# A transformer block with a routed feed-forward on one core: gathers issued in groups, and a new order of the opening steps

## The chip, the core and the metric

One core of one Trainium2 chip runs the whole program. The metric is device time in microseconds: from the start of the execution to its end, median of the runs. The profiler's page and trace come from one further execution.

## The reference, cut to what matters

Everything is float32. One layer on x (2048 rows of 512): two branches, each behind a layer norm that a modulation vector scales and shifts; all six modulation vectors come from one 512 x 3072 product.

```python
mod = (silu(c) @ wmod).reshape(1, 6, 1, 512)
sa, ca, ga, sb, cb, gb = mod[:, 0], ..., mod[:, 5]
ga = (2 * (ga >= 0) - 1) * maximum(abs(ga), 0.25)      # gb alike
h = layernorm(x) * (1 + ca) + sa
x = x + ga * (tanh(h @ B.T) @ C.T + D * h)             # 256 states
h = layernorm(x) * (1 + cb) + sb
scores = sigmoid(h @ gate_w.T)                         # 8 experts
# top 2 of scores + bias, weights normalised over the two
y = sum over the two experts of w * (silu(h @ W1) * (h @ W3)) @ W2   # 352 wide
x = x + gb * (y + shared)                              # shared: the same form, 704 wide
```

## The kernel before

**Precision.** Each float32 product is made of three TensorE passes on a high part (ScalarE's copy into the `hi` tile, type fp32r) and a low part (VectorE's or GpSimd's value minus high part, the `lo` tile): high by high, high by low, low by high. So each operand costs one ScalarE copy and one subtraction before TensorE can use it.

**Tiling.** The 2048 rows are 16 tiles of 128, worked in 8 pairs. `iterations` runs a software pipeline over `it`; at `it` the engines work on pair `it` (statistics, normalising: `first_stats`, `first_aggr`, `first_root`, `normalise`), on pair `it - 1` (transposes of the normalised tile `tbuf`: `turn_t` on TensorE, high part `turned` on ScalarE, low part `turned_low` on VectorE, then `states`), on pair `it - 2` (`attention`, which is the product with C; residual sum, second layer norm, giving `h2`), and on pair `it - 3` (transposes of `h2`, high part `high_a`, low part `lows_a`, then the first half of the shared expert: `up`, SiLU in `hidden`, product `gbuf` in `product_a`, transposes of `gbuf` in `turn_g`, high and low part `gth` and `gtl`, `down`). The term with D is added to x by GpSimd (`times_d`, `with_d`). The parameter `lo` of each `body` is the iteration's number where it is written out (0 to 4 and the last ones), so conditions such as `lo == 3` single out one of them. `body(3)` is the first with all four stages.

**Opening.** Ahead of `body(3)` each engine has its own list. TensorE forms the six modulation vectors (`modulation(0)` to `(5)`, the last in PSUM bank 7) between the first pairs' transposes, states and attention. The shared expert's weights come in three pieces: W1/W3 in two (`first_weights(0)`, `(1)`) and W2 (`first_weights(2)`), which GpSimd first multiplies by gb (L698). `guard(5)` forms that gb: VectorE takes the sign from PSUM (L1282), ScalarE the magnitude (`magnitude`), and VectorE joins them (L1285). The router's weights are 32 columns, high part L890 on ScalarE, low part L1624 on VectorE; TensorE's first `up` waits for them.

**The later stages.** Stage A's rows are scattered by expert. Stage B gives the shared expert's other half to the last four tiles, stage S takes the routed tiles through their experts (results to `ys_rows` in HBM), and stage C gives the shared expert's other half to the other 12 tiles. Each `step` is: `up`, `down` of the tile before, transposes of `gbuf`. In C each tile's two routed rows are fetched by two indirect DMAs from GpSimd (`gather`, into `tbuf` and `xtf`), with indices that VectorE makes (`offsets`) once the place is free. The six tiles that went through the shared half elsewhere or come last (`FIRST_LAST`) have their rows fetched beside, by `gather_first`, into `rowb`; ScalarE weighs the first row (`weigh`, at the steps in `WEIGH_AT`), and VectorE does three operations for each (`combine`, parts 0 to 2, at the steps in `COMBINE_AT`, numbered 3 * tile + part). The queue of each engine is in program order: a wait in it holds all that stands behind.

Of the kernel before, what the change touches and what calls it, by code (L numbers as in the profile page):

```python
# [39 lines left out]
UP = 2 * F  # L40
# [23 lines left out]
WEIGH_AT = [2, 4, 5, 7, 8, 10]  # L64
COMBINE_AT = [(), (), (), (0, 1), (2,), (3, 4), (5, 6), (7, 8), (9, 10), (11, 12), (13, 14), (15, 16)]
# [17 lines left out]
def build(nc, x, ccol, wmod, bt, ct, dvec, gwt, rb, w_all, consts, out):  # L83
# [6 lines left out]
    with ExitStack() as ctx:  # L90
# [223 lines left out]
        def pairs_of_b(eng):  # L314

            return eng.value_load(ti[0:1, TB_ITERS:TB_ITERS + 1], min_val=NP - 2, max_val=SMAX // 2 - 2) + 2

# [219 lines left out]
        def _(pool):  # L537
# [75 lines left out]
            def body(it, lo, hi):  # L613
# [87 lines left out]
            with_d(2)  # L701
# [60 lines left out]
        def _(act):  # L762
# [14 lines left out]
            def hidden(p, j, lo):  # L777
                n = p * 2 + (j + 1)
                act.wait_ge(q["A", "up"], n)
                if lo > 3 or j:  # L780
# [3 lines left out]
                               ACT.Copy).then_inc(s_lg, 1)  # L784
                if lo == NP + 1 and j == 1:
# [20 lines left out]
            def turned(p, lo):  # L806
# [3 lines left out]
                for j in range(2):  # L810
                    act.activation(thi[:, :, j * P:j * P + P],
                                   bank[2 + j][:, :].rearrange("p (k m) -> p k m", k=KD),
# [130 lines left out]
        def _(pe):  # L943
# [38 lines left out]
            def up(sec, i, j, off, there=None, loaded=None, apart=False):  # L982
# [13 lines left out]
                for m, h in [(m, h) for h in range(2) for m in range(KD)] if apart else [  # L996
# [4 lines left out]
                    if True:  # L1001
                        if sec == "A":
                            w, n = m * UPA + h * (E + F), F + (1 - h) * E
                        else:
                            w, n = off + (SH + m * UP + h * F), F
                        wh, wl = whi[:, bass.ds(w, n)], wlo[:, bass.ds(w, n)]
                        dst = bank[2 + h][:, 0:n]
# [845 lines left out]
```

## Time and profile before

| | us |
|---|---|
| median of 3 runs | 557.76 |
| lowest, highest | 556.29, 557.81 |
| the profiled execution | 561.89 |
| its span, first to last instruction | 560.2 |
| TensorE busy in it | 542.0 |
| VectorE, GpSimd, ScalarE busy | 291.0, 262.8, 176.8 |
| TensorE's mean granted clock | 0.994 of full |

The profiled execution is one of its own and need not equal the median. A row of the timeline gives start, length, engine, line of the kernel, operation, the tiles written and read, the count, and in brackets how long the engine stood idle before and what released it. The ends of matmuls are modelled. "Issue" as a releaser means nothing that the profile shows. PE is TensorE, DVE VectorE, ACT ScalarE, POOL GpSimd, SP SyncE.

### The profile page before, as it was taken

Reading aid. Unit: us, or ns where it says so; the run is one execution under the profiler, and the core shown is the slowest. Engines: PE = TensorE matmul, PEld = TensorE weight load, DVE = VectorE, ACT = ScalarE, POOL = GpSimd, SP = SyncE. Lnnn points to the kernel's source line nnn. Section 1 sums busy time; section 2 is a strip of 40 time slices with the busy share of each in tenths; the row PEclk is TensorE's granted clock in tenths of the full one; section 3 lists DMA queues with packets and bytes.
Section 4 is the critical chain, followed back from the end, with each engine's and each line's share of the span. In section 5 each row is a group of like instructions: output and inputs, shape, how many; then the busy total and the mean of one; then the engine's idle time right before and its main releaser. Section 6 shows DMA issues by size and latency. Waiting matters only on the chain.

```text
span 560.2 us, 11029 instructions
## 1 busy us (share of the span) xinstructions
PE 542.0 (97%) x3129; PEld 485.9 (87%) x3130; DVE 291.0 (52%) x612; ACT 176.8 (32%) x337; POOL 262.8 (47%) x221
## 2 busy tenths in 40 slices
PE   8997899999999999999999999999999999979997
PEld 3666888998999999899999999999999999958996
DVE  3787886696677657732222222222222221257887
ACT  1444435445443432122222223222233222112121
POOL 2499877667667457443054350053434200346530
PEclk9997999999999999999999999999999999999999
DMA  8999266543543397576354946265666413568952
GB/s 305 397 349 383 98 216 254 189 140 123 187 150 150 135 331 269 201 271 222 111 191 135 340 140 238 75 210 192 252 210 250 131 66 123 166 205 286 312 179 75
DMA packets 45676, 115.62 MB, mean 206 GB/s; under 512 B 4560, under 2 KB 4816, under 8 KB 45648
## 3 DMA queue, kind: packets, MB, share of 16 engines
q1 hardware_dynamic: 32848, 62.83, 31.9%
q0 software_dynamic: 12800, 52.43, 27.1%
q8 instruction: 16, 0.26, 0.2%
q14 instruction: 12, 0.10, 0.0%
HBM read 78.28 MB, written 36.96 MB: 206 GB/s over the span
## 4 chain that ended last, share of the span: by engine, by line
PE 88%; DVE 4%; another core or an unknown queue 2%; issue 2%; ACT 1%; DMA 1%; SPq 0%; DVEq 0%; ACTq 0%
PE bank L1010 15%; PE bank L1008 15%; PE bank L1009 15%; PE bank L1039 8%; PE bank L1041 8%; PE bank L1040 8%; PE bank L979 5%; PE bank L1046 4%; PE bank L948 3%; PE bank L949 3%; PE bank L950 3%; PE bank L957 3%; DMA x_all<-wmod 1%; DVE gtl L1301 1%
## 5 line engine op out<-in xcount | busy, mean ns | idle before, releaser
L1008 PE MATMUL bank<-whi,thi 128*128 (+2 forms) x368 | 122.8, 334 | 0.0
L580 POOL TENSOR_TENSOR wlo<-raw,whi 128x1408 f32 (+3 forms) x24 | 79.8, 3338 | 91.6 <-DMA whi<-w_all 80.7
L1009 PE MATMUL bank<-wlo,thi 128*128 (+2 forms) x368 | 119.6, 325 | 0.0
L1010 PE MATMUL bank<-whi,tlo 128*128 (+2 forms) x368 | 119.1, 324 | 0.0
L1740 DVE TENSOR_TENSOR gbuf<-s,bank 128x352 f32<-128x352 f32 x52 | 27.1, 521 | 105.2 <-ACT s L922 102.7
L1039 PE MATMUL bank<-whi,gth 128*128 (+1 forms) x201 | 79.8, 397 | 1.5 <-issue 1.5
L1041 PE MATMUL bank<-whi,gtl 128*128 (+1 forms) x201 | 79.1, 393 | 0.0
L1040 PE MATMUL bank<-wlo,gth 128*128 (+1 forms) x201 | 78.8, 392 | 0.0
L1758 DVE TENSOR_TENSOR gtl<-bank,gth 128x384 fp32r<-128x384 f32 x51 | 28.4, 557 | 84.4 <-ACT gth L929 81.3
L922 ACT ACTIVATE s<-bank 128x352 f32<-128x352 f32 x52 | 24.2, 466 | 149.8 <-PE bank L1010 143.8
L1008 PEld LDWEIGHTS bank<-whi,thi 128*128 128x128 f32 x368 | 69.7, 189 | 0.0
L1009 PEld LDWEIGHTS bank<-wlo,thi 128*128 128x128 f32 x368 | 69.1, 188 | 0.1
L1010 PEld LDWEIGHTS bank<-whi,tlo 128*128 128x128 f32 x368 | 69.1, 188 | 0.0
L929 ACT ACTIVATE gth<-bank 128x384 fp32r<-128x384 f32 x51 | 25.1, 492 | 105.7 <-PE bank L1046 97.2
L1008 PE MATMUL bank<-whi,xah 128*128 128x352 f32 (+2 forms) x176 | 58.3, 331 | 0.1
L1009 PE MATMUL bank<-wlo,xah 128*128 128x352 f32 (+2 forms) x176 | 57.2, 325 | 0.0
L1010 PE MATMUL bank<-whi,xal 128*128 128x352 f32 (+2 forms) x176 | 57.1, 325 | 0.0
L1041 PEld LDWEIGHTS bank<-whi,gtl 128*128 128x128 f32 x201 | 37.8, 188 | 8.9
L1039 PEld LDWEIGHTS bank<-whi,gth 128*128 128x128 f32 x201 | 37.9, 189 | 7.5 <-issue 1.8
L1040 PEld LDWEIGHTS bank<-wlo,gth 128*128 128x128 f32 x201 | 37.8, 188 | 5.8
L738 POOL DMA_INDIRECT tbuf<-ys_rows,idx x10 | 11.2, 1115 | 61.0 <-issue 44.3
L1046 PEld LDWEIGHTS bank<-cst,gbuf 128*128 128x128 f32 x204 | 25.7, 140 | 16.0 <-DVE gbuf L1740 4.3
(224 smaller groups left out, 984.5 us busy)
## 6 DMA issues: line engine op xcount, KB each, us to landing
raw<-w_all POOLq DMA_DIRECT2D x8, 2176.0 KB
whi<-w_all POOLq DMA_DIRECT2D x16, 704.0 KB, 11.4
h<-xs_rows SPq DMA_DIRECT2D x36, 256.0 KB, 2.8
ys_rows<-tmpa SPq DMA_DIRECT2D x36, 256.0 KB, 2.0
x_all<-wmod SPq DMA_DIRECT2D x6, 1024.0 KB, 9.3
whi<-w_all POOLq DMA_DIRECT2D x8, 768.0 KB, 5.3
hs_rows<-h SPq DMA_DIRECT2D x8, 512.0 KB, 4.9
mods<-hs_rows SPq DMA_DIRECT2D x7, 512.0 KB
```

The lines of the kernel that those rows point to most:

```text
L580: pool.tensor_tensor(wlo[:, bass.ds(off + (SH + a), b - a)], raw[:, a:b], whi[:, bass.ds(off + (SH + a), b - a)].bitcast(F32), ALU.subtrac ...
L929: act.activation(gth_b if last else gth[:, :], bank[4][:, 0:FP], ACT.Copy).then_inc(q["S", "ghi"], 1)
L979: mm = pe.transpose(dst[:, k * P:(k + 1) * P], src[:, k * P:(k + 1) * P], ident)
L1008: pe.matmul(dst, xh[:, j, a], wh, start=(m == 0), stop=False)
L1009: pe.matmul(dst, xh[:, j, a], wl, start=False, stop=False)
L1010: mm = pe.matmul(dst, xl[:, j, a], wh, start=False, stop=(m == KD - 1))
L1039: pe.matmul(dst, gth[:, a], wh, start=(m == 0), stop=False)
L1040: pe.matmul(dst, gth[:, a], wl, start=False, stop=False)
L1041: mm = pe.matmul(dst, gtl[:, a], wh, start=False, stop=(m == KF - 1))
L1046: mm = pe.transpose(dst[:, m * P:(m + 1) * P], gbuf[:, m * P:(m + 1) * P], ident)
L1740: dve.tensor_tensor(gbuf[:, 0:F], s1[:, :], bank[3][:, 0:F], ALU.mult).then_inc(q["S", "g"], 1)
L1758: dve.tensor_tensor(gtl_b if last else gtl[:, :], bank[4][:, 0:FP], (gth_b if last else gth[:, :]).bitcast(F32), ALU.subtract).then_inc(q[ ...
```

## The change

In stage C the gathers of rows (`gather_first`) are issued in the groups of `ROWS_AT`: none ahead of the first loop step, then after each tile's own gathers two, two, one, one, two, one, one and two of them, each group behind a wait for the transposes of `gbuf` of a step of stage C. `WEIGH_AT` and `COMBINE_AT` are moved one step later, and the last tile's part 1 goes into the last step, so parts 1 and 2 stand behind the last subtraction and `finish_last(0, 0, 1)`.

In the opening: on TensorE, `h2`'s transposes and the attention of pair 1 stand ahead of the transposes of pair 2, which go to banks 6 and 7 instead of 2 and 3 and wait for the states and for gb's sign and magnitude. On ScalarE, the router's high part comes before the states of pair 1, `high_a(0)` ahead of `normalise(2)`, pair 2's high part behind, and the SiLU of the first tile ahead of W2's high part. On VectorE, `h2` of pair 0 comes ahead of W1's second low part, `lows_a(0)` next, pair 3's statistics behind the first `gbuf`, `gtl` and the second `gbuf` ahead of `slo`. On GpSimd, `with_d(2)` moves from ahead of `body(3)` to behind its roots.

```diff
-WEIGH_AT = [2, 4, 5, 7, 8, 10]
-COMBINE_AT = [(), (), (), (0, 1), (2,), (3, 4), (5, 6), (7, 8), (9, 10), (11, 12), (13, 14), (15, 16)]
+WEIGH_AT = [3, 4, 6, 7, 9, 10]
+COMBINE_AT = [()] * 4 + [(n, n + 1) for n in range(0, 16, 2)]
+ROWS_AT = [(0, 1), (2, 3), (4,), (5,), (6, 7), (8,), (9,), (10, 11)]
...
+        def t_bank(lo, j):
+
+            return bank[6 + j] if lo == 3 else bank[2 + j]
@@ gpsimd @@
+                if lo == 3:
+                    with_d(2)
                 if lo > 2 and live(0, lo, hi):
                     times_d(it)
...
             times_d(2)
-            with_d(2)
             iterations(pool, body, 3)
...
             for j in range(2):
                 gather(CB, j)
-            for k in range(2):
-                gather_first(0, k)
             for c in range(CB + 1, NP - 1):
                 for j in range(2):
                     gather(c, j)
-                    n = (c - CB - 1) * 2 + j + 1
-                    if n < NB + NL:
-                        for k in range(2):
-                            gather_first(n, k)
+                    n = (c - CB - 1) * 2 + j
+                    turned_there = value(pool, iters * 2 + (NB + n + 3))
+                    pool.wait_ge(s_bidx, 2)
+                    pool.wait_ge(q["S", "gt"], turned_there)
+                    for m in ROWS_AT[n]:
+                        gather_first(m // 2, m % 2)
@@ scalar @@
+                if lo == 3 and j == 0:
+                    first_weights(2)
...
-                if live(1, lo, hi):
+                if live(1, lo, hi) and lo != 3:
                     turned(it - 1, lo)
                 if live(3, lo, hi):
                     p = it - 3
-                    if lo < NP + 2:
+                    if 3 < lo < NP + 2:
                         high_a(p, lo)
+                    if lo == 3:
+                        turned(it - 1, lo)
                     if lo > NP:
                         scores(p - 1)
-                    if lo == 3:
-                        first_weights(2)
                     hidden(p, 0, lo)
...
             modulation(4)
+            act.wait_ge(l_gate, 32)
+            act.activation(whi_a[:, :, 0:E], gw[:, :, :], ACT.Copy).then_inc(s_gwh, 1)
             states(1, 2)
+            high_a(0, 3)
             normalise(2)
             magnitude(5)
-            act.wait_ge(l_gate, 32)
-            act.activation(whi_a[:, :, 0:E], gw[:, :, :], ACT.Copy).then_inc(s_gwh, 1)
@@ tensor @@
+                if lo == 3:
+                    pe.wait_ge(s_tanh, p * 2)
+                    pe.wait_ge(s_sign, 2)
+                    pe.wait_ge(s_abs, 2)
+                for j in range(2):
+                    mm = transposes(t_bank(lo, j), tbuf[:, j, :])
...
-                if live(1, lo, hi):
+                if live(1, lo, hi) and lo != 3:
                     turn_t(it - 1, lo)
...
                 if live(2, lo, hi):
                     attention(it - 2, lo)
-
+                if lo == 3:
+                    turn_t(it - 1, lo)
...
-                    if live(1, lo, hi):
+                    if live(1, lo, hi) and lo > 3:
                         pe.wait_ge(s_tlo, (it - 1) * 2 + 2)
@@ vector @@
-                if live(3, lo, hi) and lo < NP + 2:
+                if live(3, lo, hi) and 3 < lo < NP + 2:
                     lows_a(it - 3, lo)
+                if lo == 3:
+                    turned_low(it - 1, lo)
...
                 if lo == 3:
+                    first_stats(it, lo)
+                    first_aggr(it, lo)
                     first_weights(2)
                 between(1)
+                if lo == 3:
+                    low_a(it - 3, 0, lo)
...
                     if lo == 2:
-                        first_weights(1)
                         dve.wait_ge(s_modc, 4)
...
+                if lo == 3:
+                    product_a(it - 3, 1, lo)
                 if live(1, lo, hi):
                     states_low(it - 1)
-                if live(3, lo, hi):
+                if live(3, lo, hi) and lo > 3:
                     product_a(it - 3, 1, lo)
...
             body(2, 2, 2)
-            guard(5, sign5[:, :], s_gb)
+            sign_of(5, sign5[:, :])
+            lows_a(0, 3)
+            first_weights(1)
             dve.wait_ge(l_gate, 32)
             dve.wait_ge(s_gwh, 1)
             dve.tensor_tensor(wlo_a[:, :, 0:E], gw[:, :, :], whi_a[:, :, 0:E].bitcast(F32),
                               ALU.subtract).then_inc(s_gwl, 1)
+            guard(5, sign5[:, :], s_gb)
             link(dve.memset(gbuf[:, F:FP], 0.0))
             body(3, 3, 3)
...
                     dve.wait_ge(q["S", "dn"], i * 2 + j)
                     finish_last(0, 0, 1)
-                    combine(NB + NL - 1, 2)
+                    for part in (1, 2):
+                        combine(NB + NL - 1, part)
```

`sign_of` is the first half of the old `guard`; `turned` and `turned_low` read `t_bank` too.

## Rows read from the trace of the kernel before

**Rows 1.** The page, part 1: busy time, share of the span, instructions.

```profile
PE 542.0 (97%) x3129; PEld 485.9 (87%) x3130; DVE 291.0 (52%) x612; ACT 176.8 (32%) x337; POOL 262.8 (47%) x221
```

**Rows 2.** TensorE's timeline, opening: start, length, engine, line, operation [idle before].

```profile
46.37 1.94 PE L979 MATMUL bank<-cst,tbuf 128*128 128x128 f32 x8 [3.82 <-issue]
...
53.73 0.33 PE L1008 MATMUL bank<-whi,xah 128*128 128x360 f32 x1
...
59.01 0.52 PE L1046 MATMUL bank<-cst,gbuf 128*128 128x128 f32 x3 [1.20 <-DVE gbuf L1297]
```

**Rows 3.** GpSimd's timeline in the opening.

```profile
30.91 3.64 POOL L689 TENSOR_TENSOR x_all<-x_all,tmpa 128x1024 f32<-128x1024 f32 x1
...
40.43 1.09 POOL L623 TENSOR_TENSOR rs<-ve,mhalf 128x2 f32<-128x2 f32 x1
...
47.23 2.69 POOL L596 TENSOR_TENSOR x_all<-x_all,tmpa 128x1024 f32<-128x1024 f32 x1
...
58.56 2.39 POOL L596 TENSOR_TENSOR x_all<-x_all,tmpa 128x1024 f32<-128x1024 f32 x1
```

**Rows 4.** Busy time by stretch; after POOL: TensorE's granted clock, DMA share, GB/s.

```profile
42.54:46.37 3.83, 0.01 (x2) 0.04 (x1) 2.48 (x4) 1.63 (x3) 3.61 (x6) 0.88 1.05 402
46.37:52.20 5.83, 5.83 (x22) 5.35 (x23) 5.31 (x7) 2.67 (x6) 5.75 (x3) 0.50 1.05 365
```

**Rows 5.** TensorE's timeline in stage C.

```profile
478.62 0.49 PE L1046 MATMUL bank<-cst,gbuf 128*128 128x128 f32 x3
...
484.89 0.49 PE L1046 MATMUL bank<-cst,gbuf 128*128 128x128 f32 x3
...
488.94 0.32 PE L1010 MATMUL bank<-whi,tlo 128*128 x1
...
493.01 0.55 PE L1046 MATMUL bank<-cst,gbuf 128*128 128x128 f32 x3 [1.67 <-issue]
...
502.31 0.55 PE L1046 MATMUL bank<-cst,gbuf 128*128 128x128 f32 x3 [0.95 <-DVE gbuf L1740]
...
547.35 0.49 PE L1046 MATMUL bank<-cst,gbuf 128*128 128x128 f32 x3
```

**Rows 6.** The chain of waits in order of time, 484 to 503.

```profile
485.52 6.39 another core or an unknown queue
...
492.40 5.23 another core or an unknown queue
```

**Rows 7.** GpSimd's timeline, the first and last of ten gathers in one run.

```profile
483.35 1.03 POOL L738 DMA_INDIRECT tbuf<-ys_rows,idx  x1 [41.60 <-issue]
...
495.41 0.95 POOL L744 DMA_INDIRECT raw<-ys_rows,idxb  x1 [0.30 <-issue]
```

**Rows 8.** VectorE's timeline in the opening.

```profile
34.96 1.25 DVE L1509 TENSOR_TENSOR x_all<-bank,x_all 128x512 f32<-128x512 f32 x2
...
38.14 0.25 DVE L1530 BATCH_NORM_AGGREGATE mv<-bn 128x2 f32<-128x6 f32 x2
...
40.88 1.61 DVE L1433 TENSOR_TENSOR wlo<-raw,whi 128x1408 fp32r<-128x1408 f32 x1
...
46.86 0.84 DVE L1285 SCALAR_TENSOR_TENSOR mods<-mods,sign 128x512 f32<-128x512 f32 x1 [1.83 <-ACT mods L871]
47.62 2.35 DVE L1624 TENSOR_TENSOR wlo<-gw,whi 128x32 fp32r<-128x32 f32 x1
...
50.04 1.29 DVE L1441 TENSOR_TENSOR tlo<-bank,thi 128x512 fp32r<-128x512 f32 x2
...
58.78 3.78 DVE L1433 TENSOR_TENSOR wlo<-raw,whi 128x1536 fp32r<-128x1536 f32 x1
```

**Rows 9.** DMA issues 480 to 560: count, KB each, median us to landing.

```profile
raw<-ys_rows,idxb POOLq DMA_INDIRECT x8, 5.3
```

**Rows 10.** VectorE's timeline at the end.

```profile
555.69 0.68 DVE L1685 TENSOR_TENSOR mods<-mods,x_all 128x512 f32<-128x512 f32 x1
```

More of the change, by code:

```diff
@@ L811, in turned @@
                     act.activation(thi[:, :, j * P:j * P + P],
-                                   bank[2 + j][:, :].rearrange("p (k m) -> p k m", k=KD),
+                                   t_bank(lo, j)[:, :].rearrange("p (k m) -> p k m", k=KD),
                                    ACT.Copy).then_inc(s_thi, 1)
@@ L1000, in up @@
                         pe.wait_ge(w_ready, there[m // (KD // 2)])
[L1001 to L1007, printed above, removed]
-                        pe.matmul(dst, xh[:, j, a], wh, start=(m == 0), stop=False)
-                        pe.matmul(dst, xh[:, j, a], wl, start=False, stop=False)
-                        mm = pe.matmul(dst, xl[:, j, a], wh, start=False, stop=(m == KD - 1))
+                    if sec == "A":
+                        w, n = m * UPA + h * (E + F), F + (1 - h) * E
+                    else:
+                        w, n = off + (SH + m * UP + h * F), F
+                    wh, wl = whi[:, bass.ds(w, n)], wlo[:, bass.ds(w, n)]
+                    dst = bank[2 + h][:, 0:n]
+                    pe.matmul(dst, xh[:, j, a], wh, start=(m == 0), stop=False)
+                    pe.matmul(dst, xh[:, j, a], wl, start=False, stop=False)
+                    mm = pe.matmul(dst, xl[:, j, a], wh, start=False, stop=(m == KD - 1))
                     if apart and h == 0 and m == KD - 1:
@@ L1059, in turn_t @@
                     pe.wait_ge(s_lg, (p - 3) * 2 + 2)
+                if lo == 3:
+                    pe.wait_ge(s_tanh, p * 2)
+                    pe.wait_ge(s_sign, 2)
+                    pe.wait_ge(s_abs, 2)
                 for j in range(2):
-                    mm = transposes(bank[2 + j], tbuf[:, j, :])
+                    mm = transposes(t_bank(lo, j), tbuf[:, j, :])
                 mm.then_inc(s_tT, 1)
@@ L1277, in _, with sign_of @@
                 dve.tensor_scalar(silb[k], const("ones"), sil[:, k:k + 1], None, ALU.mult).then_inc(s_silb, 1)
+            def sign_of(i, sign):
+                dve.wait_ge(s_mod, i + 1)
+                dve.tensor_scalar(sign, bank[MBANK[i]][:, :], 0.0, 0.5, ALU.is_ge, ALU.subtract).then_inc(s_sign, 1)
             def guard(i, sign, done):
-                g, m = bank[MBANK[i]][:, :], mods[:, WM[i], :]
-                dve.wait_ge(s_mod, i + 1)
-                dve.tensor_scalar(sign, g, 0.0, 0.5, ALU.is_ge, ALU.subtract).then_inc(s_sign, 1)
+                m = mods[:, WM[i], :]
                 dve.wait_ge(s_sign, 1 if i == 2 else 2)
@@ L1440, in turned_low @@
                     t = slice(j * P, (j + 1) * P)
-                    dve.tensor_tensor(tlo[:, :, t], bank[2 + j][:, :].rearrange("p (k m) -> p k m", k=KD),
+                    dve.tensor_tensor(tlo[:, :, t], t_bank(lo, j)[:, :].rearrange("p (k m) -> p k m", k=KD),
                                       thi[:, :, t].bitcast(F32), ALU.subtract).then_inc(s_tlo, 1)
@@ L1494, in between @@
                         route(it - 4, lo, *which)
-                if live(1, lo, hi) and lo > 1:
+                if live(1, lo, hi) and lo > 1 and lo != 3:
                     turned_low(it - 1, lo)
-                if live(3, lo, hi) and lo < NP + 2:
+                if live(3, lo, hi) and 3 < lo < NP + 2:
                     lows_a(it - 3, lo)
+                if lo == 3:
+                    turned_low(it - 1, lo)
                 if lo == 2:
@@ L1509, in body @@
                         dve.tensor_tensor(xt, bank[j][:, :], xt, ALU.add).then_inc(s_x1, 1)
-                if live(0, lo, hi) and lo != 2:
+                if live(0, lo, hi) and lo not in (2, 3):
                     first_stats(it, lo)
@@ L1520, in body @@
                 if live(0, lo, hi):
-                    if lo != 2:
+                    if lo not in (2, 3):
                         first_aggr(it, lo)
@@ L1571, in body @@
                     normalise(it, lo)
+                if lo == 3:
+                    product_a(it - 3, 1, lo)
                 if live(1, lo, hi):
                     states_low(it - 1)
-                if live(3, lo, hi):
+                if live(3, lo, hi) and lo > 3:
                     product_a(it - 3, 1, lo)
@@ L1606, in _ @@
             ins.then_inc(s_blo, 1)
+            sign_of(2, mods[:, 5, :])
             guard(2, mods[:, 5, :], s_ga)
```

## The prediction

> **What bounds the kernel now.** I read the page first: TensorE is busy for 542.0 of 560.2 us [rows 1], so the end moves only where TensorE waits, runs at the low clock, or has finished. The waits of TensorE and its timeline then show three such places.
>
> First the opening. TensorE stands still for 3.82 us before the transposes of pair 2 at 46.37, which wait for the normalised tile from ScalarE, and that for GpSimd's small operations behind the root that ends at 41.52 [rows 2, 3]. The granted clock falls within that idle stretch (0.88 on average) and is 0.50, the 1.2 GHz level, over 46.37 to 52.20 [rows 4]. Then come 1.20 us of waiting for the first gbuf [rows 2]. A second place is the start of the tail stage C, where results are gathered and combined. One of its steps, from the transposes of one tile's hidden row to the next one's, takes 484.89 - 478.62 = 6.27 us; the two after that take 17.42 instead of 12.54, and all ten up to 547.35 take 68.73 instead of 62.7 [rows 5]. So 4.88 us are lost in two steps and 1.15 in the other eight. The chain of waits names no engine: 6.39 and 5.23 us stand under "another core or an unknown queue" [rows 6]. The last matmul of the first product was recorded at 488.94 to 489.26 [rows 5], but ScalarE, which waits for its semaphore, went on only when that first piece ended, at 491.91. In that stretch GpSimd issues ten gathers back to back, 483.35 to 496.36 [rows 7]. The third place is the last few microseconds, VectorE's own.
>
> **The change, opening.** The sum follows the port that VectorE and GpSimd fight for. An operation of VectorE on two SBUF tiles does not run beside one of GpSimd's: the router weights' low part, 32 columns, took 2.35 us and ended at 49.97, when GpSimd's 2.69 us addition at 47.23 had ended (49.92); W2's low part took 3.78 us and ended 1.62 us after GpSimd's addition at 58.56 did [rows 3, 8]. The other way round, GpSimd's addition took 3.64 us at 30.91 where 2.39 is usual [rows 3].
>
> Step 1: h2 of pair 0 no longer waits behind W1's second low part (1.61 us, 40.88 to 42.49) [rows 8], but only for GpSimd's root at 41.52 [rows 3]. It ends some 0.8 us sooner, near 43.0, and slo follows. TensorE ends the last modulation at 42.55 and so waits about 0.4 us, then has the transposes of h2 and the attention of pair 1 to do. That cover of 4 us is what fills the 3.82 us. Pair 2's transposes come third. Even at the low clock all three blocks took 53.73 - 46.37 = 7.36 us [rows 2], so TensorE is ready for the first up product by 43.0 + 7.4 = 50.4.
>
> Step 2: what that product then waits for is the router weights' low part. GpSimd's small operations end up to 0.6 us sooner, as VectorE holds the port less. The D term in two parts follows, and near 47.23 - 0.6 = 46.6 both want the port: GpSimd for the 2.4 us addition, VectorE for W1's low part (1.61), which now stands there. If VectorE goes first, the addition ends at 46.6 + 1.5 + 2.4 = 50.5; if GpSimd does, the low part ends at 49.0 + 1.6 = 50.6. Either way the router's low part is there near 50.5. If it slipped in before the addition it would be 48.2, and 50.5 is the end that the row of 2.35 us is nearest to. So the product starts near 50.6 against 53.73.
>
> The Trainium skill (SBUF — State Buffer, section "Who interferes with whom") calls this an exclusive lock held for the whole instruction, with whoever starts first the winner. That speaks against the placing, because the guard of gb, moved behind the weights, reads two SBUF tiles too. By the rule it starts after the addition and the opening gains what step 3 gives; were the port only shared, router's part and guard would be done by 49.1, the addition near 50.5 would set the pace, and the opening would gain 4.4.
>
> Step 3: VectorE is now the late one. From 50.5: guard 0.84 [rows 8], low part of pair 2's transposes 1.29, then residual, statistics and aggregation of pair 1, 34.96 to 38.39 = 3.43 in the same order [rows 8]. That is 56.1. The first up product took 53.73 to 57.81 = 4.1 us [rows 2], so it ends near 54.7 and the SiLU is ready at 55.2, hidden by VectorE. gbuf takes 0.52, and the transposes of it begin near 56.7 instead of 59.01 [rows 2]: **2.3 us gained**. The wait in front of them grows from 1.2 to about 2.0 us.
>
> Step 4: is it kept? Statistics of pair 3 (1.5 us) precede W2's low part; that now meets only GpSimd's small operations, since its D addition has moved behind them: 1.6 us instead of 3.78, ending near 60. ScalarE's W2 high part needs W2 scaled, which starts with the guard (51.4) and takes 3.5: 54.9, after the SiLU, hence the new order of these two. With the old order the SiLU would be 1.5 us late. The down product stands 7 us behind the transposes of gbuf and so is not reached before 63.8. The D addition ends near 66 and is first needed at about 71. SP's store of h2 and the two loads of x are issued at the same waits. Nothing of this is late, so 2.3 us are kept. Bounds: 4.5 gained (router's part at 48.2 and the guard with it), 1 lost (below, the clock).
>
> **The change, stage C.** The gathers of rows start one step later, each waits for a transposed gbuf, and they are spread over eight steps (2, 2, 1, 1, 2, 1, 1, 2) instead of six twos. So the first run of ten becomes four, a pause of 2 us for tile 2's indices, four, and four more. The waits sit on GpSimd's queue behind the tile's own gathers; the next tile's indices come from VectorE some 4.4 us after that same transposition, and two row gathers take 2.5, so no tile gather is held up. A gather's landing takes 5.3 us [rows 9]; the weighing on ScalarE sits behind it in front of the next SiLU. For the first row pair, issued near 493.2 and 494.5 on the old clock, it lands at 499.8, is weighed by 500.6, and the SiLU is due at 501.6: 1 us of cover, and about as much for the others. If that cover is gone, a SiLU is late by the excess.
>
> What the calmer issue is worth the trace of before does not show. Lower end: nothing, if the lateness of the semaphores is not of the gathers. Upper end: all 6.0 us. Later, with eight gathers in a run with one short pause, steps lost only 1.15 us in eight, and the new pattern is nearest to that: two steps would lose 0.3 to 0.9 instead of 4.88, so 4.0 gained. But the profiled execution took 561.89 us (1.69 around the span), 4.13 above the median of 557.76, and this stall is the likeliest thing to be smaller without it. I take 2.5.
>
> **The end.** The last tile's second part moves behind the last subtraction: one more operation of 0.68 us [rows 10] in VectorE's chain, on the path to the last store. One is taken from no other place on the path. **0.7 us lost.** The rest costs nothing on the path: the sign is only taken apart from the guard, and the router's high part on ScalarE (32 columns) falls while TensorE still forms the states that ScalarE needs next. If its load landed late, ScalarE would hold the states of pair 1 for as long, and h2's transposes with it.
>
> **Sum.** In the profiled execution: 561.89 - 2.3 - 4.0 + 0.7 = 556.3. For the timed runs: 557.76 - 2.3 - 2.5 + 0.7 = 553.7.
>
> **The rivals.**
> (a) The stall of stage C stays, as it is not of the run of gathers; only the opening gains. For it: no engine is named, and eight later gathers in one run did little harm. Against it: the step before the gathers takes its 6.27 us and the first two with them 17.42. 557.76 - 2.3 + 0.7 = 556.2, at the edge of what counts.
> (b) The stall goes wholly in the timed runs too, and the router's part slips in early: 557.76 - 4.5 - 4.9 + 0.7 = 549.1; with the stall alone gone, 551.3.
> (c) Slower: the low clock moves. TensorE now has waits of 0.4, 0.5, 2.2 and 2.0 us within 14 us where it had 3.8 and 1.2. If the clock falls in the 2.2 us in front of the first up product, that product takes 8.2 instead of 4.1 us and part of the next block its double: about 5.5 us against the 2.3, so 3.2 lost in the opening. It decides only if the fall comes there and stage C gives nothing: 557.76 + 3.2 + 0.7 = 561.7. Waits of up to 1.67 us in stage C left the clock at full; 3.82 did not [rows 2, 5]. The 2.2 lies between.
> (d) The weighing comes late: a row gather lands 2 us later than the median once its queue is full, six times, each 1 us past its cover. Then SiLUs give back the gain: about 558.
>
> **How the numbers follow.** The forecast, opening kept and stage C better by 1 to 4 us, gets 0.45 and gives 552 to 555.5. (a) gets 0.24, (b) 0.12, (c) 0.07, (d) and other orderings that turn out no better 0.12. What this kernel's measurement can tell from no change is 0.3%, or 1.7 us: faster means under 556.1. The forecast and (b) are faster, and nearly half of (a): 0.67. Within: the rest of (a) and half of (d): 0.20. Slower, above 559.4: (c) and half of (d): 0.13. The range 549.8 to 558.6 leaves out the best of (b), (c) and the worst of (d).
>
> **What would show it.** In the profile after: TensorE's order of h2, attention, pair 2, with no idle stretch above 2.5 us near 42 to 57 and the granted clock at 1.00 there; the router's low part ending with GpSimd's addition, near 50.5; the first gbuf transposes near 56.7 (58 or later proves step 3 wrong, 54.6 proves the lock wrong). In stage C: steps of about 6.3 us from the first on and no piece of 5 us under an unknown queue; if these pieces stand while gathers are fewer, (a) is right. At the end, eight operations of VectorE after the last subtraction where seven were, 0.7 us longer. The prediction fails if the clock falls before the first up product, or if ScalarE waits for a row's landing.

## The result, and the profile of the changed kernel

The changed kernel takes **553.61 us** (553.57 to 556.34, 6 runs) against 557.78 (556.29 to 559.44, 6 runs) for the kernel before on the same chip: a ratio of 0.9946, 95% interval 0.9931 to 0.9961. Timed again with the experiments below it gave 553.57 (0.9933, 0.992 to 0.9946). The forecast was 553.7. The sum hit the total, and that is luck: two of its terms were each wrong by over 2 us, in opposite directions. Most of what follows is about that.

| | us |
|---|---|
| profiled execution, its span | 556.34, 554.6 |
| TensorE busy in it | 540.5 |
| VectorE, GpSimd, ScalarE busy | 293.1, 263.0, 176.5 |
| mean granted clock | 0.995 |

The changed kernel's runs fall in two groups, and the profiled one is of the upper: spans of about 551.9 with a granted clock of 0.999 or 1.0 (four of six), and about 554.6 at 0.995 (two of six).

TensorE's timeline in the opening, every entry that has an idle time ahead of it (start, length, engine, line, operation, [idle before <- releaser]):

```profile
43.58 1.06 PE L988 MATMUL bank<-cst,h 128*128 128x128 f32 x8 [0.61 <-issue]
47.80 1.07 PE L988 MATMUL bank<-cst,tbuf 128*128 128x128 f32 x8 [0.34 <-ACT mods L879]
50.55 0.42 PE L1016 MATMUL bank<-whi,xah 128*128 128x360 f32 x1 [1.68 <-issue]
57.42 0.52 PE L1054 MATMUL bank<-cst,gbuf 128*128 128x128 f32 x3 [1.20 <-DVE gbuf L1312]
69.80 1.06 PE L988 MATMUL bank<-cst,h 128*128 128x128 f32 x8 [1.80 <-DVE gtl L1316]
```

The idle stretch of 3.82 us [rows 2] is gone, and the first up product starts at 50.55 instead of 53.73. But it is followed by the low clock, which takes most of the gain in this execution (busy time by stretch; behind POOL the granted clock):

```profile
50.50:54.20 3.70, 3.65 (x13) 3.69 (x14) 3.56 (x7) 0.00 (x0) 3.07 (x1) 0.54 1.01 384
```

VectorE's timeline in the opening, the lines that answer to [rows 8]:

```profile
48.11 2.33 DVE L1649 TENSOR_TENSOR wlo<-gw,whi 128x32 fp32r<-128x32 f32 x1
50.37 0.68 DVE L1300 SCALAR_TENSOR_TENSOR mods<-mods,sign 128x512 f32<-128x512 f32 x1
...
55.10 0.25 DVE L1547 BATCH_NORM_AGGREGATE mv<-bn 128x2 f32<-128x6 f32 x2
56.76 0.52 DVE L1312 TENSOR_TENSOR gbuf<-s,bank 128x352 f32<-128x352 f32 x1 [1.41 <-ACT s L788]
...
58.73 1.73 DVE L1448 TENSOR_TENSOR wlo<-raw,whi 128x1536 fp32r<-128x1536 f32 x1
...
62.35 3.45 DVE L1583 SCALAR_TENSOR_TENSOR h<-h,rs,mods 128x512 f32<-128x512 f32 x2
...
66.16 2.43 DVE L1472 TENSOR_TENSOR slo<-st,shi 128x512 fp32r<-128x512 f32 x1
```

And GpSimd's: the last addition of pair 1's D term, and the first two operations of pair 2's (`with_d(2)`, which the change moves here):

```profile
46.78 3.61 POOL L601 TENSOR_TENSOR x_all<-x_all,tmpa 128x1024 f32<-128x1024 f32 x1
...
62.26 3.00 POOL L598 TENSOR_TENSOR tmpa<-tmpa,a 128x512 f32<-128x512 f32 x2
```

W2's low part takes 1.73 us where it took 3.78. The last two of VectorE's lines are new: two operations on SBUF tiles that take 3.45 and 2.43 us beside GpSimd's moved D term, where the same operations took 1.41 and 0.68 in the kernel before. They will matter.

Stage C on TensorE, the first and the last of ten steps and the one with a delay:

```profile
478.00 0.49 PE L1054 MATMUL bank<-cst,gbuf 128*128 128x128 f32 x3
484.26 0.49 PE L1054 MATMUL bank<-cst,gbuf 128*128 128x128 f32 x3
...
503.22 0.55 PE L1054 MATMUL bank<-cst,gbuf 128*128 128x128 f32 x3
...
541.05 0.49 PE L1054 MATMUL bank<-cst,gbuf 128*128 128x128 f32 x3
```

The ten steps take 541.05 - 478.00 = 63.05 us, not the 68.73 of the kernel before (547.35 - 478.62) [rows 5]. No piece of the chain stands under "another core or an unknown queue". In this pair of profiles the change thus saves 0.6 us by the start of stage C (478.62 - 478.00), 5.7 in its ten steps, and loses 0.7 at the end: 5.6, as the spans say (560.2 - 554.6). That looks like a success of the gathers. It isn't, as the experiments show.

### The profile page after: what moved, and what is told of

Its sections match the earlier page's. It is cut to its first block, busy times and chain, and to the rows that moved or that the text cites. A ratio compares the mean times of both kernels' runs of the same rounds, so it can differ in the third digit from the quotient of the medians.

```text
span 554.6 us, 11046 instructions
## 1 busy us (share of the span) xinstructions
PE 540.5 (97%) x3129; PEld 485.6 (88%) x3130; DVE 293.1 (53%) x612; ACT 176.5 (32%) x337; POOL 263.0 (47%) x221
## 3 DMA queue, kind: packets, MB, share of 16 engines
q1 hardware_dynamic: 32848, 62.83, 32.3%
## 4 chain that ended last, share of the span: by engine, by line
PE 83%; DVE 5%; issue 1%; ACT 1%; DVEq 0%
PE bank L1016 15%; PE bank L1017 15%; PE bank L1018 15%; PE bank L1047 8%; PE bank L1049 8%; PE bank L1048 8%; PE bank L1054 4%; PE bank L988 4%; PE bank L957 2%; PE bank L959 2%; PE bank L958 2%; DVE gtl L1316 1%; DVE st L1669 0%; DVE slo L1472 0%; ACT gth L800 0%
## 5 line engine op out<-in xcount | busy, mean ns | idle before, releaser
L1016 PEld LDWEIGHTS bank<-whi,thi 128*128 128x128 f32 x368 | 69.8, 190 | 0.0
L556 POOL DMA_DIRECT2D whi<-w_all x21 | 11.4, 552 | 54.8 <-PE bank L1018 54.7
```

What stands on the lines that cost most here:

```text
L1016: pe.matmul(dst, xh[:, j, a], wh, start=(m == 0), stop=False)
```

## The experiments

In what follows "first" and "second gbuf" are the transposes of gbuf for the two tiles of pair 0, "h2 of pair 1" the transposes after them, "ten steps" the stretch read from [rows 5].

**The two halves apart.** First the new opening with the old order of gathers and sums, then the old opening with the new one, the kernel before once more, and the changed kernel with the first row pair gathered ahead of the loop again.

```diff
# e1_opening_only: the changed kernel, with
-WEIGH_AT = [3, 4, 6, 7, 9, 10]
-COMBINE_AT = [()] * 4 + [(n, n + 1) for n in range(0, 16, 2)]
+WEIGH_AT = [2, 4, 5, 7, 8, 10]
+COMBINE_AT = [(), (), (), (0, 1), (2,), (3, 4), (5, 6), (7, 8), (9, 10), (11, 12), (13, 14), (15, 16)]
...
# the old loop of gather_first and the old last step; e2_gathers_only: the reverse, on the kernel before
# e4_first_pair_back: the changed kernel, with
-ROWS_AT = [(0, 1), (2, 3), (4,), (5,), (6, 7), (8,), (9,), (10, 11)]
+ROWS_AT = [(), (2, 3), (4,), (5,), (6, 7), (8,), (9,), (10, 11)]
             for j in range(2):
                 gather(CB, j)
+            for k in range(2):
+                gather_first(0, k)
```

> The changed kernel with stage C as before: the opening alone. Theory (the two parts add up, and stage C gave 5.7 us in the profile): stage C's ten steps take about 68.7 us again, the time is 555.5 to 558, about 1 us under before. Rival (the opening gives most of what the timed runs gained, and the stall of stage C was the profile's): 553.5 to 554.5, and stage C near 63 us in most executions.

> The kernel before with the new gathers, weighing and combining alone. Theory: stage C's ten steps take 63.0 us, the end 0.7 us more, so 5.0 us less in the profile; in the timed runs 3 to 5 us under before. Rival (the stall is hardly there in timed runs): within 1 us of before.

> The kernel before, as it was, to see each execution's span and granted clock. If the low clock in the opening comes and goes, spans fall in groups about 2 to 3 us apart with mean clocks near 0.994 and 1.0. If the stall of stage C is there in each execution, the profile has it again (ten steps 68 to 69 us); if it comes and goes, this profile may show about 63.

> The changed kernel, but the first pair of row gathers stands ahead of the loop again, so six to eight gathers are issued in one run at the start of stage C. Theory (the length of that first run makes TensorE's semaphores late): the pieces under an unknown queue are back, stage C's ten steps take 67 to 69 us, 4 to 5 us slower than the changed kernel. Rival (the number of row gathers in later steps, or something else, is the cause): stage C stays near 63 us and the time near 553.6.

| | us | runs | ratio to before, 95% interval | ten steps in its profile |
|---|---|---|---|---|
| before, beside them | 557.52 | 20 | | |
| e1, opening alone | 552.87 | 5 | 0.994 (0.9916 to 0.9964) | 62.83 |
| e2, gathers alone | 558.55 | 10 | 1.0021 (1.0008 to 1.0034) | 63.38 |
| e3, before again | 557.41 | 10 | 0.9996 (0.9986 to 1.0005) | 62.83 |
| e4, first pair back | 553.31 | 4 | 0.9931 (0.9914 to 0.9948) | 62.83 |

The opening alone gives the whole gain and more: 4.65 us. The new gathers alone cost 1.0. The kernel before, profiled again, has its run of ten gathers and no stall at all: 62.83 in ten steps. So the stall of 4.88 us belonged to the one execution that had been profiled first, 4.13 us above its median. Over all thirteen later profiles the ten steps take 62.83 to 63.80, and eight of these have the old run of ten gathers. That the gathers can never bring such a stall is not shown; that they don't bring it in a usual execution is. e4 says the same from the other side: with eight gathers in one run at the start of the changed kernel, where 67 to 69 us were expected in ten steps, these take 62.83.

The second profile of before (557.29 us, near the median) also shows another opening than the first. TensorE:

```profile
46.42 1.94 PE L979 MATMUL bank<-cst,tbuf 128*128 128x128 f32 x8 [3.82 <-issue]
57.70 0.52 PE L1046 MATMUL bank<-cst,gbuf 128*128 128x128 f32 x3 [1.20 <-DVE gbuf L1297]
66.25 0.47 PE L1039 MATMUL bank<-whi,gth 128*128 128x512 f32 x1 [1.23 <-DVE gtl L1301]
69.28 0.55 PE L1046 MATMUL bank<-cst,gbuf 128*128 128x128 f32 x3 [0.67 <-DVE gbuf L1297]
71.09 1.06 PE L979 MATMUL bank<-cst,h 128*128 128x128 f32 x8 [0.40 <-DVE gtl L1301]
```

VectorE and GpSimd beside it:

```profile
57.48 2.68 DVE L1433 TENSOR_TENSOR wlo<-raw,whi 128x1536 fp32r<-128x1536 f32 x1
60.08 3.55 DVE L1547 SCALAR_TENSOR_TENSOR h<-x_all,mv,mods 128x512 f32<-128x512 f32 x2
64.22 1.41 DVE L1563 SCALAR_TENSOR_TENSOR h<-h,rs,mods 128x512 f32<-128x512 f32 x2 [0.59 <-POOL rs L623]
```

```profile
58.62 3.79 POOL L596 TENSOR_TENSOR x_all<-x_all,tmpa 128x1024 f32<-128x1024 f32 x1
```

And the opening alone (e1), on TensorE:

```profile
50.50 0.40 PE L1015 MATMUL bank<-whi,xah 128*128 128x360 f32 x1 [1.69 <-issue]
55.85 0.52 PE L1053 MATMUL bank<-cst,gbuf 128*128 128x128 f32 x3 [1.20 <-DVE gbuf L1311]
66.83 1.06 PE L987 MATMUL bank<-cst,h 128*128 128x128 f32 x8 [0.39 <-DVE gtl L1315]
```

By the first gbuf the gain is 57.70 - 55.85 = 1.85 us; by h2 of pair 1 it is 71.09 - 66.83 = 4.26. So 2.4 us, more than half, come between the two. As the rows read, the kernel before loses them there to GpSimd's D term: W2's low part takes 2.68, the first half of h2 3.55 where 1.41 is usual, the root behind the addition is awaited, and gtl, last in VectorE's queue, reaches TensorE 1.23 us late.

The first profile of before, the one that the prediction was made from, doesn't have this loss. Its h2 of pair 1 follows the first gbuf (59.01) by 10.97 us, as in e1 (10.98), not by 13.39:

```profile
69.98 1.06 PE L979 MATMUL bank<-cst,h 128*128 128x128 f32 x8 [0.39 <-DVE gtl L1301]
```

There the low clock had lasted twice as long, and VectorE came to W2's low part at 58.78, when GpSimd had just started its addition at 58.56 [rows 3, 8]. It lost to it once (3.78 us), and both halves of h2 then took 1.4 each. In e3 it came at 57.48, 1.3 us sooner, met GpSimd twice, and h2 of pair 1 was 1.1 us later for it. So in the kernel before a fall of the clock in the opening costs little or nothing: of its executions timed beside the experiments, the two with a granted clock of 1.0 took 557.25 and 557.28, and the fastest (556.1 to 556.7) all had 0.993 or 0.994, as the first profile with its long low stretch.

**Is the moved D term what gives the 2.4 us?** From here on the base is e1, and the kernel before beside these runs took 557.75 (19 runs).

```diff
# e5_d_term_back
-                if lo == 3:
-                    with_d(2)
...
             times_d(2)
+            with_d(2)
             iterations(pool, body, 3)
```

> The new opening with the old stage C (as in the opening alone, 552.87 us), but GpSimd adds pair 2's D term ahead of its roots again. Theory (the moved D term is worth about half of the opening's gain, since W2's low part, h2 of pair 1 and the D term then fight for one port): the second tile's down product or gbuf waits again, 1 to 2 us together, h2's transposes of pair 1 come 1.5 to 3 us later than 66.8, time 554.4 to 556. Rival (the new order of TensorE's blocks gives all of it): 552.6 to 553.2.

Measured 559.53 (558.51 to 560.22, 8 runs; ratio 1.0033, 1.0021 to 1.0044): 6.7 us above e1 (6.4 if each is taken against the kernel before beside it), 3.5 above the upper end of what was expected, and slower than the kernel before. The wait moved to the second gbuf, on TensorE:

```profile
70.42 0.55 PE L1052 MATMUL bank<-cst,gbuf 128*128 128x128 f32 x3 [3.38 <-DVE gbuf L1310]
```

On GpSimd the addition at 60.01 takes 3.79 us and everything for pair 1's root stands behind it until 65.6; behind that wait TensorE ran at the low clock again. With two falls of the clock in the profile, 6.7 is not the price of the place beside VectorE alone. But the direction is plain: without this edit the new order loses.

**The router's low part first.** 

```diff
# e6_router_early
             sign_of(5, sign5[:, :])
-            lows_a(0, 3)
-            first_weights(1)
             dve.wait_ge(l_gate, 32)
             dve.wait_ge(s_gwh, 1)
             dve.tensor_tensor(wlo_a[:, :, 0:E], gw[:, :, :], whi_a[:, :, 0:E].bitcast(F32),
                               ALU.subtract).then_inc(s_gwl, 1)
+            lows_a(0, 3)
+            first_weights(1)
```

> The new opening with the old stage C, and the low part of the router's weights ahead of the two low parts of h2 on VectorE. Theory (VectorE's chain behind the guard sets the first gbuf, not the router's part): the first up product starts near 49 instead of 50.5, and the transposes of gbuf stay within 0.3 us of 55.85; time 552.6 to 553.3, or up to 2.5 us more if the longer wait in front of those transposes takes the clock down. Rival (the router's part sets it): 1.5 us faster, about 551.3.

Measured 554.53 (554.51 to 555.1, 4 runs; 0.9951, 0.9934 to 0.9968). The up product now starts without a wait, 2.2 us earlier (48.26), and the first gbuf only 0.33 earlier:

```profile
55.52 0.64 PE L1053 MATMUL bank<-cst,gbuf 128*128 128x128 f32 x3 [3.10 <-DVE gbuf L1311]
```

So a sooner up product alone doesn't bring the first gbuf; VectorE's chain, from the end of GpSimd's addition to the aggregation, holds it, as step 3 of the prediction had it. (e12 will add that a sooner VectorE alone doesn't bring it either.) And the whole wait in one piece, 3.10 us, is followed by the low clock, which the 1.20 of e1 was not:

```profile
55.70:59.20 3.50, 3.50 (x19) 3.50 (x18) 3.41 (x7) 0.58 (x2) 3.42 (x4) 0.51 0.37 136
```

**The states of pair 2 in the wait.**

```diff
# e7_states_first
+                if lo == 3:
+                    states(it - 1, lo)
...
-                if live(1, lo, hi):
+                if live(1, lo, hi) and lo != 3:
                     states(it - 1, lo)
```

> The new opening with the old stage C, and on TensorE the states of pair 2 ahead of the transposes of the first gbuf, in the time in which it waits for them. Theory (that wait of 1.20 us is on the path and nothing behind it becomes late): the wait is gone, 1.0 to 1.3 us faster, 551.6 to 551.9, and the low clock comes less often. Rival (VectorE and GpSimd set the pace behind it as well): the wait shows up at the second gbuf or at h2 of pair 1 instead, 552.6 to 553.

Median 554.24 of ten runs (0.995, 0.9926 to 0.9974), in three groups: five at 552.4 to 552.9 with the clock at 0.999 or more, two at 555.6 to 555.8 (0.996), three at 556.5 to 557.2 (0.994). The best are 0.3 us under e1's, where 1.0 to 1.3 were expected. The wait moved to the second gbuf (0.92 us at 64.64), and the falls of the clock are no rarer (five of ten runs, against two of five). Filling this wait gives next to nothing, as VectorE is late again one tile on.

**SiLU behind W2's high part, as before.**

```diff
# e8_w2_before_silu
-                if lo == 3 and j == 0:
-                    first_weights(2)
...
+                    if lo == 3:
+                        first_weights(2)
                     hidden(p, 0, lo)
```

> The new opening with the old stage C, but ScalarE makes W2's high part ahead of the first SiLU again. Theory (it waits for GpSimd's scaled W2 until 54.6 and then takes 1.5): the SiLU comes at 56.1 instead of 54.7, the first gbuf's transposes 1.2 us later than 55.85, time 553.9 to 554.2. Rival (VectorE is late anyway): within 0.3 us of 552.87.

Measured 555.47 (555.24 to 555.97, 6 runs; 0.9964, 0.9951 to 0.9976), 2.6 above e1. The first gbuf is 1.28 us later (57.13, behind 2.58 us of waiting), as expected; but 553.9 to 554.2 were expected for the time. The clock is low from 58.16 on, and the rest of the loss is the meeting described under e12.

**The chain shortened.** e6, with the first gbuf taken ahead of pair 1's statistics.

```diff
# e9_gbuf_before_stats: e6, with
                         dve.tensor_tensor(xt, bank[j][:, :], xt, ALU.add).then_inc(s_x1, 1)
+                if lo == 3:
+                    product_a(it - 3, 0, lo)
...
-                if live(3, lo, hi):
+                if live(3, lo, hi) and lo > 3:
                     product_a(it - 3, 0, lo)
# e12_gbuf_first_alone: e1, with the same edit
```

> Base: the new opening with the old stage C, 552.87 when timed. Two edits: the router's low part ahead of pair 0's low parts on VectorE, as in the run of that edit alone (554.53, transposes of the first gbuf at 55.52 behind a wait of 3.10 us for gbuf, which drew a fall of the clock), and the first gbuf ahead of the statistics of pair 1 instead of behind them. My theory: VectorE's chain sets the first gbuf transposes, 1.5 us of it being those statistics, and the length of the wait in front of them decides whether the clock falls. Then gbuf is formed at about 53.3 us, as soon as its SiLU is there, its transposes begin near 54.0 with a wait of 1.3 us, the clock stays at full in most runs, and the time is 551.0 to 552.4. The rival: what is late afterwards is h2 of pair 1, whose statistics come 0.6 us later, and the next product's weights; TensorE only waits there instead, 552.6 to 554.5.

```profile
53.93 0.52 PE L1053 MATMUL bank<-cst,gbuf 128*128 128x128 f32 x3 [1.38 <-DVE gbuf L1311]
```

**552.12 us** (551.96 to 552.24, 4 runs) against 557.5 (11 runs): 0.9904, 0.9889 to 0.9918. It is the best of the kernels, 1.45 us under the changed kernel beside it, and its granted clock was 0.999 or 1.0 in every run. The same edit without the router's:

> Base: the new opening with the old stage C (552.87 when timed, two of five runs near 555.2 with the granted clock at 0.996). One edit: the first gbuf ahead of the statistics of pair 1 on VectorE. With the router's low part ahead as well, this gave 552.12 and no fall of the clock in the opening. Theory: the falls come from the wait of 1.69 us in front of the first up product, and that wait is still here, so some of the runs still stand 2.3 to 2.7 us higher, with a low stretch that begins within 0.5 us of that product's start; at full clock the first gbuf transposes stay within 0.3 us of 55.85, as now the SiLU, ready at about 55.0, decides. Median 552.5 to 553.5 with single runs at 555 or more. The rival: it is the wait for gbuf that decides on the clock, as in the kernel with 3.10 us there; then all runs stand within 0.5 us of 552.5.

**557.97** (556.41 to 558.68, 11 runs; 1.0007, 0.9995 to 1.0019): five us worse than e1, where both theories expected 552.5 to 553.5. Its profile has the first gbuf at 55.85 exactly as e1, at full clock, though VectorE is ready for it 1.6 us sooner. It waits for the SiLU instead, which is ready at 55.14:

```profile
55.18 0.52 DVE L1311 TENSOR_TENSOR gbuf<-s,bank 128x352 f32<-128x352 f32 x1 [1.62 <-ACT s L787]
```

In e1 the aggregation ends at 55.31 and the SiLU at 55.15, so both chains held the first gbuf, and only both edits together (e9) bring it. What differs is further on. VectorE's second half of h2 in e12, and GpSimd's D term beside it:

```profile
62.29 3.45 DVE L1584 SCALAR_TENSOR_TENSOR h<-h,rs,mods 128x512 f32<-128x512 f32 x2
...
66.09 2.41 DVE L1471 TENSOR_TENSOR slo<-st,shi 128x512 fp32r<-128x512 f32 x1
```

```profile
62.20 2.99 POOL L597 TENSOR_TENSOR tmpa<-tmpa,a 128x512 f32<-128x512 f32 x2
```

The same in e1:

```profile
60.78 1.43 DVE L1582 SCALAR_TENSOR_TENSOR h<-h,rs,mods 128x512 f32<-128x512 f32 x2
...
64.63 0.69 DVE L1471 TENSOR_TENSOR slo<-st,shi 128x512 fp32r<-128x512 f32 x1
```

```profile
62.22 2.55 POOL L597 TENSOR_TENSOR tmpa<-tmpa,a 128x512 f32<-128x512 f32 x2
```

GpSimd's D term starts at the same time in both, but not for the same reason. In e1 GpSimd does its last small operations beside h2's second half, and the D term starts when that half has ended (60.78 + 1.43 = 62.21). In e12 VectorE comes to the second half 1.5 us later, because the statistics now wait behind a gbuf that waits for its SiLU. GpSimd has its small operations behind it when h2's first half ends, at 62.19, and the D term goes in between the two halves. In the first order h2's second half costs 1.43 us; in the other it costs 3.45, and slo behind it 2.41 instead of 0.69. By gtl this has made VectorE 2.9 us late (69.02 against 66.12), and so is h2 of pair 1:

```profile
69.71 1.84 PE L987 MATMUL bank<-cst,h 128*128 128x128 f32 x8 [2.06 <-DVE gtl L1315]
```

and its wait, 2.06 us, is followed by the low clock in that profile. This is read from the rows; no run takes the D term out of e12. But all ten profiles with the moved D term show the same two orders, here sorted by the first column:

| | h2's second half starts | D term starts | h2 of pair 1 on TensorE |
|---|---|---|---|
| e4 | 60.30 | 61.74 | 66.35 |
| e9 | 60.38 | 61.82 | 66.19 |
| e6 | 60.44 | 61.88 | 68.67 |
| e7 | 60.65 | 62.09 | 66.45 |
| e1 | 60.78 | 62.22 | 66.83 |
| changed kernel again (e11) | 60.92 | 62.36 | 66.97 |
| e10 | 61.86 | 61.77 | 69.31 |
| e8 | 62.05 | 61.96 | 69.58 |
| e12 | 62.29 | 62.20 | 69.71 |
| changed kernel | 62.35 | 62.26 | 69.80 |

The D term starts either 1.44 us behind h2's second half, which is when that half is over, or 0.09 ahead of it, and nowhere between: it is a cliff. With the one order h2 of pair 1 comes at 66.2 to 67.0, with the other at 69.3 to 69.8. e6 is the exception: its order is the good one, but with the fall of the clock behind its long wait, and slo at 2.15 us beside GpSimd's addition, h2 of pair 1 is 1.8 us later than in e1 all the same.

So e9's statistics are early enough only because its router's low part lets the product, and thus the SiLU, come 2.2 us sooner. Neither edit is worth anything alone; e6 loses, e12 loses more.

**The end, and the changed kernel again.**

```diff
# e10_end_as_before: the changed kernel, with
-COMBINE_AT = [()] * 4 + [(n, n + 1) for n in range(0, 16, 2)]
+COMBINE_AT = [()] * 4 + [(n, n + 1) for n in range(0, 14, 2)] + [(14, 15, 16)]
...
-                    for part in (1, 2):
-                        combine(NB + NL - 1, part)
+                    combine(NB + NL - 1, 2)
```

> The changed kernel whole, but with part 1 of the last tile's weighed sum back in the last step ahead of the last subtraction, as before, so one operation of 0.7 us fewer stands at the end. Theory: the end is VectorE's alone, so 0.7 us come back: last transposes of stage C to the end of the span 12.9 us instead of 13.55, and the time is 0.5 to 0.8 below the changed kernel of this call (about 552.9). The rival: the subtraction of the last tile then comes later by as much on VectorE's queue, and nothing changes.

> The changed kernel once more, unchanged, beside the other two on the same chip. Theory: its times stand in two groups, 553.0 to 554.0 with the granted clock at 0.999 or above and 556 to 556.6 with one fall of the clock (0.995 to 0.996); the profile's ten steps of stage C take 62.8 to 63.4 us, and no step above 7 us. If the stall of 4.9 us in stage C that the one profile of the kernel before showed were a thing of chance that any kernel can meet, one of these profiles could show it too.

e11 gave 553.57 (553.4 to 554.33, 5 runs). e10 gave 554.41 (552.91 to 556.26, 6 runs), three of them behind a fall of the clock, where about 552.9 was expected. So the medians say nothing on the edit; the three at a clock of 0.999 or more, 552.91, 553.05 and 553.21, stand some 0.5 under the three lowest of e11 (553.4, 553.54, 553.57). Part of the 0.7 comes back, with too few runs to say how much. In e10's profile the last transposes but one of stage C stand 13.24 us before the end of the span, in e11's 13.58, and in e9's, which keeps the old order there, 12.89.

Their profiles show the late weighing too. ScalarE waits for a landing of a first row pair in front of the fourth step's SiLU, in e11

```profile
499.46 0.81 ACT L915 ACTIVATE raw<-raw,zrow,wts 128x512 f32<-128x512 f32 x1 [4.02 <-DMA raw<-ys_rows,idxb]
```

and that step takes 6.81 us instead of 6.30 (7.18 in e10, 6.87 in e2, 6.39 in the changed kernel's first profile). In e4, where the first pair is fetched earlier, no weighing waits like that and all ten steps take 62.83.

## Why the prediction came out right, and which steps were wrong

The total was right because two errors cancelled, which is luck. The opening was worth twice what the sum said (4.65 us in e1, not 2.3), and stage C nothing (not 2.5).

**Step 1 and step 2** held. h2's transposes start at 43.58 after 0.61 us (0.4 expected), the blocks are in the expected order, and the router's low part ends at 48.11 + 2.33 = 50.44, with GpSimd's addition (50.39); 50.5 was expected. Its 32 columns take 0.89 us in e9 where GpSimd is not in the way, and 2.33 here. The rule weighed in the prediction, from the Trainium skill (SBUF — State Buffer, section "Who interferes with whom"), agrees with that and with the guard behind it, which starts at 50.37. In e6 it is the guard that takes 2.88.

**Step 3** held within 0.7 us. The aggregation ends at 55.35 against 56.1: the guard took 0.68 and the residual, statistics and aggregation 52.33 to 55.35 = 3.0, where the rows gave 0.84 and 3.43. At full clock the first gbuf is at 55.99 (e11), 0.7 sooner than the 56.7 of the sum, behind a wait of 1.2 where 2.0 was expected; the product ends at 54.8, as said (54.7). What the step had wrong is that the SiLU is hidden by VectorE with 0.9 us to spare (55.2 against 56.1): in e1 the two end 0.16 us apart, and e12 shows that the SiLU holds the first gbuf as much. Against the profiled execution of before (59.01) this gains 3.0 us, against the second profile (57.70) 1.7. The 2.3 lies between, by luck.

**Step 4 is the term that was mis-sized.** It kept the 2.3 us of the first gbuf and asked only whether anything would become late behind it. The opening gave 4.65 in timed runs. Against the profiled execution e1 gains 3.2 us at the first gbuf (59.01 - 55.85) and the same 3.2 at h2 of pair 1 (69.98 - 66.83): that much was step 3 coming out better than said. The other 1.1 us up to h2 of pair 1 (71.09 - 69.98) is what e3 loses to the D addition at its old place and the profiled execution did not. No row that the prediction had shows it, as TensorE waited only 0.39 us there. What the rows did show was that the D addition stretched W2's low part to 3.78 us, and so that the old place was in VectorE's way. The step took a gain from one execution and subtracted it from a median over others, whose openings ran differently. Nor did it see that the moved D term meets h2's second half: "near 66 and first needed at about 71" is true of the addition and leaves out what it costs VectorE.

**Stage C's step failed outright.** 2.5 us were expected in timed runs, with 0.7 lost at the end. e2 shows the new gathers with the new end 1.0 slower than the old, and the changed kernel (e11) is 0.7 slower than e1, so the gathers gained nothing. The stall was of one execution. This is what rival (a) says of stage C, and its argument, that no engine was named, pointed the right way. The prediction knew that the profiled execution was 4.13 us above the median, and that the stall was 4.88 and 6.0 in all, and still gave a run of the median a share in it. An excess of the profile over the median, and a stall of that size in the profile, are most simply the same thing. The second profile bears that out: the first is 4.6 us longer (560.2 against 555.6), 5.9 of them in the ten steps, less the 1.3 by which its stage C started sooner. The late weighing, rival (d), is there, but in one step and not six: 0.1 to 0.9 us.

**The end** was right: 13.55 us from the last transposes but one to the end, against 12.85, so 0.70 (0.68 expected).

**The clock, rival (c)**, holds in its place and not in its price. In the profiled execution the fall comes 0.25 us into the first up product, behind the 1.68 us wait, where it was feared. The low stretch lasts 3.41 us and delays the first gbuf by 57.42 - 55.99 = 1.43, not 4. The rest of the 2.7 us between the two groups of runs is the cliff: VectorE comes 1.4 us later to h2's second half, the D term goes in ahead of it, and h2 of pair 1 is 69.80 - 66.97 = 2.8 late. None of e11's five runs shows such a fall (0.999 or 1.0).

Put together for timed runs: the opening -4.65 (e1) and the gathers with the end +1.03 (e2) make -3.6, where -4.2 and -3.9 (e11) were measured. So the two halves add up to within 0.6 us.

**What stays open.** Why semaphores of TensorE came late in the one execution of the kernel before (2.65 us for the product that is recorded to end at 489.26) isn't known; no later profile showed it again, so nothing could be tried on it. Nor is it shown what decides, from run to run, whether the clock falls behind a wait of 1.7 us. That two runs of e11 took 554.3 at full clock fits the late weighing (its profile is one of them), but the other has no profile.

## What to carry to other kernels

When a profiled execution lies several us above the median, profile the kernel once more before a stall in it is given a price, and before a gain read from it is subtracted from the median. When an operation is moved to another place in its queue, follow the waits behind its old place as far as they go, and list what it meets in its new place; what sits within a microsecond of another engine's start there can be a cliff, as here, and a small delay upstream, one fall of the clock included, is then paid twice. An order that shortens one wait may be worth nothing until the chain behind it is shortened too, as the router's low part and the first gbuf here: alone they lost some 1.5 and 5 us against e1, together they gained 0.7.

## What the runs showed of the hardware

Every low stretch of the clock in the opening lasted 3.41 us in these profiles (50.80 to 54.21 in the changed kernel's first, granted clock 0.50), save the 6.83 of the first profile of before. With TensorE's waits of 2.58 us and more (2.58, 3.10, 3.38, 3.82 twice, 4.22 in e2) came one each, in the wait or up to 1.0 us behind it. With waits of 1.7 to 2.1 us it came in some executions (e5, e10, e12 and the changed kernel's first) and not in others (e1, e4, e7, e11). With waits of 1.4 us or less it never came.

VectorE and GpSimd on SBUF tiles hold each other up in both directions, and the one that is second waits until the other's operation has ended: 32 columns took 0.89 us or 2.33 (e9, e1), h2's second half 1.43 or 3.45 (e1, e12), GpSimd's addition of 128x1024 2.39 or 3.79 (before, e3), by who had started. GpSimd's small operations pay too: a 128x2 root took 0.70 us in e12, ahead of W2's low part, and 2.15 in e11, beside it.
